# A selective scan with its layer behind it: delta's high part stored twice, transfers in the order of their data, decay units ahead of the outer products

## What is computed

```python
A = -exp(A_log)                                # [256, 32]
deltaBC = einsum('bld,od->blo', x, W_bc)       # 64 + 32 + 32 columns: dt_r, B, C
delta = softplus(dt_r @ W_dt.T + b_dt)
dA  = exp(delta_t[:, :, None] * A[None])
dBu = (delta_t * u_t)[:, :, None] * B_t[:, None, :]
h   = dA * h + dBu
y_t = einsum('bdn,bn->bd', h, C_t)
```

## Time and profile before

| | |
|---|---|
| time, median of 3 runs | 958.17 us (947.65 to 995.27) |
| profiled execution | 962.21 us, of which its span is 960.1 us |
| PE busy | 850.7 us (89%) |
| DVE busy | 758.1 us (79%) |
| ACT busy, POOL busy | 503.7 us (52%), 460.2 us (48%) |
| mean granted TensorE clock | 0.865 |

### The profile page before, as it was taken

How to read it: one execution, slowest core, us unless ns; L and a number is a source line. 1 busy time by engine, 2 the same in 40 slices (tenths; PEclk the granted TensorE clock), 3 DMA queues, 4 the chain that set the end, 5 groups by cost and what they waited for, 6 DMA issues and landing times.

```text
span 960.1 us, 21876 instructions
## 1 busy us (share of the span) xinstructions
PE 850.7 (89%) x7436; PEld 631.8 (66%) x7436; DVE 758.1 (79%) x773; ACT 503.7 (52%) x897; POOL 460.2 (48%) x782
## 2 busy tenths in 40 slices
PE   5568999999899898989998999997999878999985
PEld 4457665766666566667666766775766547887874
DVE  8704994998599869967986688997589937899884
ACT  4216754676557647654765466774345234445531
POOL 6404652564265446534652465573124624466344
PEclk9767995999799979985997589998589869999997
DMA  2971774577449638754964496487435332200101
GB/s 63 200 159 54 120 211 100 121 123 228 127 95 180 169 89 126 222 126 106 136 200 116 90 150 168 100 128 219 95 77 115 108 113 88 74 23 23 45 23 66
DMA packets 245313, 114.59 MB, mean 119 GB/s; under 512 B 166864, under 2 KB 238032, under 8 KB 245200
## 3 DMA queue, kind: packets, MB, share of 16 engines
q1 hardware_dynamic: 238864, 109.16, 49.7%
q10 hardware_dynamic: 6336, 3.93, 1.5%
HBM read 58.43 MB, written 54.62 MB: 118 GB/s over the span
## 4 chain that ended last, share of the span: by engine, by line
PE 43%; DVE 17%; SPq 15%; issue 10%; ACT 5%; POOL 4%; DMA 4%; DVEq 0%; ACTq 0%; POOLq 0%
DVE arena L1813 11%; PE psum L1352 8%; PE psum L1422 8%; PE psum L429 7%; PE psum L1340 7%; PE psum L1429 7%; SPq L983 4%; SPq L974 4%; SPq L966 3%; ACT arena L1562 2%; SPq L991 2%; PE psum L1281 2%; POOL arena L370 2%; SPq L998 2%; PE psum L1274 2%
## 5 line engine op out<-in xcount | busy, mean ns | idle before, releaser
L1813 DVE TENSOR_TENSOR_SCAN arena<-arena,psum 128x1024 f32<-128x1024 f32 x256 | 568.9, 2270 | 147.3 <-PE psum L1429 134.9
L1562 ACT ACTIVATE arena<-psum 128x512 f32<-128x512 f32 x512 | 280.4, 597 | 278.5 <-PE psum L1340 273.3
L1219 POOL TENSOR_TENSOR carry<-arena 128x64 f32<-128x64 f32 x252 | 109.5, 434 | 318.7 <-ACT arena L1562 146.8
L1340 PEld LDWEIGHTS psum<-delta_mov,a_sta 96*128 96x128 bf16 x2048 | 142.8, 109 | 167.3 <-issue 104.8
L1422 PE MATMUL psum<-du_mov,b_sta 96*128 96x128 bf16 x2048 | 179.6, 238 | 38.3 <-DVE arena L1813 22.8
L1340 PE MATMUL psum<-delta_mov,a_sta 96*128 96x128 bf16 x2048 | 183.0, 237 | 21.3 <-ACT arena L1562 15.8
L1422 PEld LDWEIGHTS psum<-du_mov,b_sta 96*128 96x128 bf16 x2048 | 142.1, 108 | 64.0 <-DVE arena L1813 35.8
L1352 PE MATMUL psum<-arena,c_sta 128*32 128x512 f32 x1024 | 168.5, 729 | 1.7 <-ACT y_rows L1569 1.7
L1429 PE MATMUL psum<-carry,ident 128*128 128x32 f32 x1024 | 168.2, 291 | 0.1
L1429 PEld LDWEIGHTS psum<-carry,ident 128*128 128x128 f32 x1024 | 154.5, 217 | 0.3 <-POOL carry L1217 0.3
L429 PE MATMUL psum<-delta_mov,arena 128*128 128x256 f32 (+6 forms) x544 | 117.7, 376 | 7.1 <-ACT arena L550 7.1
(11 more groups left out here) (177 smaller groups left out, 841.3 us busy)
## 6 DMA issues: line engine op xcount, KB each, us to landing
du_mov<-du_terms SPq DMA_DIRECT2D x128, 192.0 KB
du_terms<-arena SPq DMA_DIRECT2D x42, 512.0 KB, 6.7
y<-y_rows SPq DMA_DIRECT2D x32, 256.0 KB
delta_terms<-arena SPq DMA_DIRECT2D x48, 128.0 KB, 5.2
delta_mov<-delta_terms SPq DMA_DIRECT2D x128, 48.0 KB
b_sta<-b_terms SPq DMA_DIRECT2D x128, 48.0 KB
b_terms<-small SPq DMA_DIRECT2D x42, 128.0 KB, 2.1
arena<-in_L_attn_x SPq DMA_DIRECT2D x8, 512.0 KB, 3.6
```

What stands on the lines that cost most here:

```text
L1219: ins = pool.tensor_tensor(carry[:, g, :], seg[:, :, 0], before[:, :, TS - 1], ALU.mult)
L1340: mm = nc.tensor.matmul(psum[:, (4 + u % 2) * BANK + i * P:(4 + u % 2) * BANK + (i + 1) * P], a_sta[0:ROWS, dg * P:(dg + 1) * P], sub(delt ...
L1562: nc.scalar.activation(sub(arena, 0, P, u * 16 * TS, (TS, 16), (decay_at(k, 1), SUBS), (1, TS)), sub(psum, 0, P, (4 + u % 2) * BANK, (TC, ...
L1813: nc.vector.tensor_tensor_scan(arena[:, STATE_AT[s] + o:STATE_AT[s] + o + GD * TS], arena[:, decay_at(k, s) + o:decay_at(k, s) + o + GD * TS],
```

## The change

**The store and the load of delta.** The part list of the stored delta becomes four entries, `D_ENTRIES = (0, 1, 0, 2)`: high, middle, high, low. Entries 0 to 2 and entries 1 to 3 together are the six terms, so `load_md` needs one DMA per quarter, 4 instead of 12; its memory side has the dimensions [2, 12, 2048], and its other side 24 partitions. `A_STATION` puts A's parts into the matching terms. There are 8 stores of delta per tile instead of 6.

**The order of transfers.** At kk = 2 SP issues the stores of B and then the load of the next tile's delta, and the stores of du after them; before, the stores of du stood first. B's stores move there from kk = 0. The high part of du is waited for apart from the others. At the start only the first chunk's quarter of each part is stored ahead of the first load, the second chunk's delta too, and the rest goes out behind it.

**PE's order.** In a step the decay units come first, ahead of the outer products. `units_at` gives two units per step to kk = 3 too, two to each of the first two steps of a tile, and in kk = 0 from step 2 on 2, 0, 2, 2, 3, 3. The sixteen B and C products are made four at a time at n = 0, 2, 4, 6, and C's transpose moves to the last step of the tile before. Before the first scan 12 units are made instead of 4. ACT and POOL have their pieces at other steps accordingly.

```diff
 STATION_PART = (0, 0, 0, 1, 1, 2)
-RUNS = ((0, 3), (3, 2), (5, 1))
+D_ENTRIES = (0, 1, 0, 2)
+A_STATION = (0, 0, 1, 1, 2, 0)
 ROWS = DQ * TERMS * B
 QROWS = TERMS * B
         AHEAD = 2
-        FIRST_UNITS = UNITS // GROUPS
+        FIRST_UNITS = 3 * UNITS // GROUPS
 
         def units_at(first, kk, step):
 
-            if first and kk == 0 and step < GROUPS - 1:
-                return [(0, (step + 1) * FIRST_UNITS + i) for i in range(FIRST_UNITS)]
-            if first and kk == 0 and step == GROUPS - 1:
-                return [(1, i) for i in range(2 * UNITS_PER_STEP)]
-            if kk == 0 and step < AHEAD:
-                return []
-            if kk == CT - 1 and step >= AHEAD:
-                edges = (0, 3, 6, 9, 12, 14, UNITS)
+            if first and kk == 0 and step < AHEAD:
+                return [(0, u) for u in range(FIRST_UNITS, UNITS)] if step == 0 else []
+            if kk == 0 and step >= AHEAD:
+                edges = (0, 2, 2, 4, 6, 9, 12)
                 return [(1, u) for u in range(edges[step - AHEAD], edges[step - AHEAD + 1])]
             at = (step - AHEAD) % STEPS * UNITS_PER_STEP
             return [(int(step >= AHEAD), at + i) for i in range(UNITS_PER_STEP)]
             return t.rearrange("p (b n) -> p b n", b=B)
 
-        MD_LOADS = DQ * len(RUNS)
+        MD_LOADS = DQ
         MU_LOADS = 8
-        D_STORES = 2 * PARTS
+        D_STORES = 2 * len(D_ENTRIES)
+        D_LATER = D_STORES * (CT - 1)
+        HI_TERMS = MOVING_PART.count(0)
-            def store_delta(p, k, s, done):
+            def store_delta(p, e):
                 for h in range(2):
-                    sp_.dma_start(dram(delta_terms_d, (p * PARTS + s) * (B * CT * D * TC) + h * P * TC,
+                    sp_.dma_start(dram(delta_terms_d, (p * len(D_ENTRIES) + e) * (B * CT * D * TC) + h * P * TC,
                                        (TC, P), (D * TC, B * CT), (1, TC)),
-                                  dparts[k][s][:, h * BANK:(h + 1) * BANK].rearrange("p (c t) -> p c t", t=TC))\
-                        .then_inc(S[done], 16)
             def load_md(lt, cc):
                 k = cc % 2
                 for q in range(DQ):
-                    for row, parts in RUNS:
-                        sp_.dma_start(sub(delta_mov[k], q * QROWS + row * B, parts * B, q * TC * DG, (1, TC * DG)),
-                                      dram(delta_terms_d, lt * (PARTS * B * CT * D * TC) + (cc * D + q * DG) * TC,
-                                           (CT * D * TC, parts * B), (1, TC * DG))).then_inc(md_loaded[k], 16)
+                    sp_.dma_start(sub(delta_mov[k], q * QROWS, QROWS, q * TC * DG, (1, TC * DG)),
+                                  dram(delta_terms_d, lt * (len(D_ENTRIES) * B * CT * D * TC) + (cc * D + q * DG) * TC,
+                                       (B * CT * D * TC, 2), (CT * D * TC, 3 * B), (1, TC * DG)))\
+                        .then_inc(md_loaded[k], 16)
 
             def load_du(c, k):
@@ -1033,11 +1062,13 @@
                         sp_.wait_ge(base_stored[1], 16 * p)
                         load_x(lt + 2, 1)
                     if late and kk == 2:
-                        for part, ready in ((0, "uhi_ready"), (2, "ulo_ready"), (1, "umid_ready")):
-                            settle(sp_)
-                            sp_.wait_ge(S[ready], p)
-                            store_du(p, part)
-                    if not (last and kk >= 2):
+                        settle(sp_)
+                        sp_.wait_ge(S["args_ready"], (c + 1) * UNITS)
+                        store_b(p, NEW, "b_stored")
+                        settle(sp_)
+                        sp_.wait_ge(S["d_stored"], 16 * D_STORES * p)
+                        load_md(p, 0)
+                    elif not (last and kk >= 2):
                         settle(sp_)
                         sp_.wait_ge(S["args_ready"], (c + 1) * UNITS)
                         load_md(lt + (kk + 2) // CT, (kk + 2) % CT)
@@ -1054,16 +1085,27 @@
...
                     if late and kk == 1:
                         settle(sp_)
+                        sp_.wait_ge(S["dhi_ready"], p)
+                        store_delta(p, 0)
+                        store_delta(p, 2)
+                        settle(sp_)
                         sp_.wait_ge(S["dmid_ready"], p)
-                        store_delta(p, NEW, 0, "d_stored")
-                        store_delta(p, NEW, 1, "d_stored")
+                        store_delta(p, 1)
+                    if not (first and kk == 0):
+                        store_y(c - 1)
+                    if late and kk == 1:
                         settle(sp_)
                         sp_.wait_ge(S["dlo_ready"], p)
-                        store_delta(p, NEW, 2, "d_stored")
-                    if not (first and kk == 0):
-                        store_y(c - 1)
-                    if late and kk == 0:
-                        store_b(p, NEW, "b_stored")
+                        store_delta(p, 3)
+                    if late and kk == 2:
+                        for part, ready, done in ((0, "uhi_ready", "uhi_stored"), (2, "ulo_ready", "u_stored"),
+                                                  (1, "umid_ready", "u_stored")):
+                            settle(sp_)
+                            sp_.wait_ge(S[ready], p)
+                            store_du(p, part, done)
+                            if part == 0:
+                                settle(sp_)
+                                sp_.wait_ge(S["b_stored"], 16 * TERMS * p)
                     if early and kk == 3:
                         store_base(lt + 2, 1)
                     if not (last and kk >= 2):
...
                             settle(sp_)
-                            sp_.wait_ge(S["u_stored"], 16 * TERMS * p)
+                            sp_.wait_ge(S["uhi_stored"], 16 * HI_TERMS * p)
+                            settle(sp_)
+                            sp_.wait_ge(S["u_stored"], 16 * MIDLO_TERMS * p)
                         load_du(c + 2, k)
 
...
@@ -1356,17 +1401,25 @@
                             start=(pi == 0), stop=(pi == SETS * SUBS - 1), skip_group_check=True)
                 return mm
 
-            def own_piece(p, n):
-
-                if n == 0:
+            def next_piece(p, n, early):
+
+                if n == CT * STEPS - 1:
                     pe.wait_ge(S["ct_ready"], p + 1)
+                    if early:
+                        pe.wait_ge(S["z_taken"], 2 * p + 4)
+                    else:
+                        pe.wait_ge(S["duT_taken"], 2 * p + 2)
                     c_transpose(NEW, 7, 2 * P)
 
             def late_piece(p, n):
 
-                if n == 0:
-                    pe.wait_ge(S["z_taken"], 2 * p + 2)
-                    cb_products(NEW, 7)
+                if n in (0, 2, 4, 6):
+                    if n == 0:
+                        pe.wait_ge(S["z_taken"], 2 * p + 2)
+                        pe.wait_ge(S["c_ready"], p)
+                    mm = cb_batch(NEW, 7, n // 2)
+                    if n == 6:
+                        mm.then_inc(S["bc_psum"], 1)
                 if n in (8, 10):
...
+
+                            for ahead, u in units_at(first, kk, step):
+                                if ahead and last and kk == 3:
+                                    continue
+                                if ahead and u == 0:
+                                    pe.wait_ge(md_loaded[1 - k], 16 * MD_LOADS * (2 * lt + (kk + 1) // 2 + 1))
+                                mm = decay_args(c + ahead, (k + ahead) % 2, u, True)
+                                if start and not ahead:
+                                    spare(1, 6)
 
                             if not (start and step < 2):
                                 pe.wait_ge(S["scan_done"], G - 1)
...
-                                if ahead and u == 0:
-                                    pe.wait_ge(md_loaded[1 - k], 16 * MD_LOADS * (2 * lt + (kk + 1) // 2 + 1))
-                                mm = decay_args(c + ahead, (k + ahead) % 2, u, True)
-                                if start and not ahead:
-                                    spare(1, 6)
```

141 lines of the change are left out of this document (88 added, 53 removed).

## The result

The changed kernel takes 1034.87 us (median of 4 runs, 1023.5 to 1070.43), the kernel before 959.92 (4 runs beside it). In some executions of either kernel the granted clock is lower and the time some per cent longer, and all ratios here leave those out. The ratio is 1.0716, with a 95% interval of [1.0521, 1.0911]: slower by some 7%. The profiled execution took 1025.0 us, its span is 1022.9.

A forecast was written before the change was run, and what follows sets the result against it. Two DMA engines carrying the narrow delta_mov load were to bound each tile: 962 + 88 (tiles 1 to 6) + 12 (tile 0) + 3 (last tile) - 7 (start) = 1058 us. Range for 8 in 10: 955 to 1125.

The forecast's parts named there:

- The narrow load: Load of delta_mov, two outermost: claimed to run on two engines and occupy both for 9.6 us a chunk.
- The bound: First two DMA engines: 101.4 us of work in a tile lasting 87 us now, so they become the bound; 0.79.
- The rival that I folded into the forecast, the clock: PE's waits for loads may drop its clock; hidden under the DMA bound, making a tile 105 to 112 us, not 102.
- the loads are spread: Rival, chance 0.14: delta_mov loads use more engines, DMA is not near its bound, tile 76 us, together 868 us.
- two engines fit and nobody waits: Rival, chance 0.07: the two engines' true work is nearer 88 us; no change, 960 us, between 940 and 977.
- The second copy: High part of delta stored twice: two more stores of 128 KB, 2.9 us of DMA work a tile.
- PE's order and spread: Decay units earlier and sixteen products split up on PE: by itself worth 7 to 12 us a tile, taken as 10.
- The branch hole stays: PE's 2.62 us hole at the loop's branch between tiles was to remain as it was.
- The start: Before and in the first chunk: load some 10 us earlier, gain 7 us, bounds 0 and 16.5.
- Tile 0's other chunks: Last three chunks of tile 0, 69.7 us before, were to become 82, +12 us.
- tiles 1 to 6 were forecast +88: Middle tiles were to go from 87.3 to 102 us, 14.7 more in each of six.
- "10 us a tile" of waits for loads: Sign in the profile after: PE waiting for DMA of delta_mov and du_mov some 10 us a tile or more.

The follow-up runs named there:

- e9: Changed kernel whole, with only the delta_mov load of a tile's fourth chunk moved behind three delta stores (six transfers): 1058.32 us, ratio 1.0985.
- e1: Changed kernel with each quarter of delta_mov loaded by two DMAs of 12 rows outermost (eight per load) instead of one: 970.42 us, ratio 1.028 to the kernel before.
- e8: Changed kernel with delta's parts stored once, six stores and twelve loads as before the change: 950.04 us, ratio 1.0016 to the kernel before.
- e4: Kernel before with only the four delta entries and 8 stores a tile, loaded by eight wide DMAs a chunk: 986.62 us, ratio 1.0433.
- e3: Kernel before with only the decay units moved ahead of the outer products of their step: 994.86 us, ratio 1.0504.
- e12: Kernel before with only the loop over the five middle tiles written out: 954.7 us, ratio 0.9867.
- e11: Changed kernel with delta's parts stored once (as e8) and the loop over the five middle tiles written out: 892.76 us, ratio 0.934 to the kernel before.
- e5: Changed kernel with the wide load of e1 and the decay units behind the outer products: 963.69 us, ratio 1.0184 to the kernel before.
- e10: Changed kernel with delta's parts stored once (as e8) and the decay units at the end of the step: 935.89 us, ratio 0.975 to the kernel before.
- e6: Changed kernel with the wide load of e1 and all sixteen units of a tile's first chunk made before the branch: 995.79 us, ratio 1.0501 to the kernel before.
- e7: Changed kernel with the wide load of e1, sixteen units made before the branch and units behind the outer products: 1018.6 us, ratio 1.0725 to the kernel before.

## Why the prediction came out as it did

The direction was right, 1058 against 1034.87 us, inside the range. The cause named first, the narrow load, is the larger part of the loss. The route by which it was to cost time was wrong, and errors of both signs partly cancelled, so the closeness of the number is in part luck. By its own steps:

**The narrow load: right in kind, too dear in size.** Two engines carry it (share 0.13), as read from y's store. It takes 8 us, not 9.6, since an engine moved 25 GB/s, more than any of the three rows that the estimate used; the prediction's other rate, 24 GB/s from the slices, was the better one. With 8 in place of 9.6 the sum of the first two engines is 95 us and the tile about 96. That this is near the measured 97.7 proves nothing of the sum, since the waits are not where it puts them. The issue of the load was to be 3.1 us shorter, and was 1.5 to 2: one of its DMAs went out every 0.85 us, not every 0.39.

**The bound: the step that failed.** I forecast that two engines are full, that everything queues behind them and that PE waits 10 us a tile for its loads. PE's waits for delta_mov in tiles 1 to 6 came to 6.8 us in all. What the runs show in its place: the 8 us stand in SP's order of transfers, and either the delta stores behind them or the load itself is late (e9). Behind the late stores ScalarE waits, PE stops for 1.5 to 3.8 us in four of the six tiles, and the clock is at its lower level for much of the chunk afterwards: 23.9 to 27.7 us for a third chunk of 17.4. The busy time of single engines isn't in the trace. In 21 of the 586 us of tiles 1 to 6 no packet was under way, and in 9 only one, so both engines can have been full for at most 95% of the time; how full they were stays open. The rival that I folded into the forecast, the clock, carries a large part of the price: in the fourth tile 0.75, against 0.92 in the earlier trace rows.

**The rivals.** That the loads are spread is excluded by the share of 0.13; that two engines fit and nobody waits, by the 42 us that e1 gave back.

**The second copy: "2.9 us" of DMA work, 25 us measured** (e1 to e8), 41 in the old order (e4). I priced the bytes and not the place. In the old order eight transfers in place of six stand ahead of y's store (e4: PE waited 11.3 us for the copy of y). In the new order six in place of four do, and eight in place of six stand ahead of a conversion on ScalarE; there the route is not shown.

**PE's order and spread: "7 to 12 us a tile; I take 10".** Within the changed kernel this gain is not to be seen (e8 equals the kernel before), and the one part of it tried by itself lost 48 us (e3). Once the branch is gone the change's orders are worth nearly that: 84.3 - 77.5 = 6.8 us a tile in tiles 1 to 5 between e12 and e11, with 10.5 us gained in the fourth chunk and the rest given back in the first two. A second step that failed is "The branch hole stays": in the fourth tile the hole grew from 2.6 to 3.9 us, and the first chunks went from 25.4 us to 27.8 (e8) and 30.0 (after). The decay units behind the branch don't make the hole longer, since it is about as long in e5 and e10, where the outer products come first (1.6 to 4.8 us). The units' place costs 5 points with the old orders (e3). In the new order of transfers its effect is small: with the new spread 1 point (e5 against e1, overlapping), and with the old spread e6 is 2 points ahead of e7, but in the profiled executions only by e7's last tile, while the first seven tiles of e6 took 14 us longer.

**The start: "-7" was wrong in sign, +12 measured.** The load did go out 12.7 us earlier, at 38.95 instead of 51.65, but PE could start on its units only 4.5 us earlier, at 53.24 instead of 57.70. And behind it stand the sixteen further stores, and du's load behind these:

```profile
38.95 2.75 SPq L989 DMA_DIRECT2D delta_mov<-delta_terms  x4
41.74 19.89 SPq L973 DMA_DIRECT2D delta_terms<-arena  x16
61.74 0.42 SPq L998 DMA_DIRECT2D du_mov<-du_terms  x1
```

PE waited 9.5 us for B's load (5.1 before) and, in the first chunk, 11.1 us for the second chunk's delta:

```profile
87.95 1.03 PE L1385 MATMUL psum<-delta_mov,a_sta 96*128 96x128 bf16 x8 [11.12 <-DMA delta_mov<-delta_terms]
```

I had counted SP's queue for the first load and not for what stands behind it. **Tile 0's other chunks** were forecast 12 us longer and were 5.8 shorter (63.9 against 69.7), and tiles 1 to 6 were forecast +88 and came to +62.8. Against the profiled 1025.0 us the forecast is 33 high: 25 in these six tiles, 18 in tile 0, 5 each in the last tile and behind the scans, less the 19 by which the start was too low.

Of the things to look for, the "10 us a tile" of waits for loads did not come: 1.1 us a tile. The share, the rate (49 to 53 GB/s, at the top of "35 to 50"), the clock (0.82), the mean share (0.53 to 0.57) and the third chunk came as forecast. The block of sixteen products is gone, and so are the regular steps of idle time in the fourth chunk. The fourth tile's fourth chunk is long for another reason: DVE waits 2.29 and 1.51 us in its first steps, where the low clock of the third chunk still holds, and 6.17 us at the branch behind it:

```profile
480.61 2.29 DVE L1874 TENSOR_TENSOR_SCAN arena<-arena,psum 128x1024 f32<-128x1024 f32 x1 [6.17 <-PE psum L1491]
```

## What to carry to other kernels

Before you merge transfers, look at the outermost dimension of each: here 96 KB in a pattern of [2, 12 rows] moved at 50 GB/s, and eight transfers of 48 KB were 42 us of kernel time faster than four of 96. Price a transfer by what stands behind it in its queue and who waits for that, not by its bytes. And before calling a reordering worthless, look whether one fixed stop (here the loop's branch with the low clock behind it) eats what it gains: writing five iterations out was worth 1.3% to the old order, which can't be told from nothing, and 7% to the new one, both with the old storage. New orders and written out loop together make the fastest kernel of the study, 893 us.

## What was not expected of the hardware

- TensorE's clock makes small stops expensive. Behind a hole of 3.9 us the granted clock was 0.51 for a chunk of 32.4 us, and a first chunk without the hole ran at 1.00 in 20.0 us (e11, tile 4, with the old storage): 12 us for a stop of four. Of five waits of PE for the same load in e12, those of 1.55, 2.34 and 1.88 us were followed by the lower level and those of 1.07 and 1.29 us were not.
- The hole at the branch is longer in the changed kernel: 2.8 to 4.4 us against 2.2 to 2.8 before, by the same branch. Why was not settled; the written out loops (e11, e12), programs longer by four copies, showed no such hole at the borders of those tiles.
- Issuing stops for a while behind a narrow transfer. Of the six delta stores behind the narrow load the second took SP 6.62 us, and all six 12.73 us. In e8, behind a load of twelve wider DMAs, the second took 1.20 us and four took 4.32 us. The same is seen behind y's store, on four engines: there the second of two delta stores took 4.19 us in the changed kernel and 3.97 in e8, and 8.26 in e9, where a narrow load and y's store both stand ahead of it. Narrow transfers are not the only cause: the second of e9's first six stores took 3.67 us behind loads of B and du alone. The Trainium skill ("DMA: Bandwidth & Descriptors", section on why a DMA increments its semaphore by 16) says that such transfers share the lowest engines; the slower issue agrees with it but does not prove it.
